# Attention probabilities times values: eight fp32r matmuls a head, or four plain float32 ones over four column quadrants

## The reference

```python
q, k, v = x @ Wq.T, x @ Wk.T, x @ Wv.T          # x is normalised; 16 heads of 32
scores = jnp.where(causal, q k^T / sqrt(32), min)
probs  = softmax(scores)                         # 512 x 512 for each head
attn   = (probs v) @ Wo.T
mod    = 0.1 * tanh(attn @ A)                    # A: 512 x 16
gate   = silu(h @ W_in.T + mod * (h @ A) @ B)
out    = residual + tanh(g) * ((gate * (h @ W_up.T)) @ W_down.T)
```

## Time and profile before

| | before |
|---|---|
| median of 3 runs | 1038.49 us (1037.32 to 1039.15) |
| the profiled execution | 1034.66 us, its span 1032.9 us |
| PE busy | 1005.7 us (97%) |
| DVE busy | 702.4 us (68%) |
| ACT busy | 603.7 us (58%) |
| POOL busy | 279.2 us (27%) |
| granted clock of PE | 1.0 of full speed in the profile |

### The profile page before, as it was taken

One profiled execution on the slowest core, in us unless ns is written; L12 is line 12 of the kernel. 1 busy time (PEld: TensorE's weight loads), 2 busy tenths in 40 slices (PEclk: granted clock), 3 DMA queues, 4 the chain that ended last, 5 costly groups with the idle time before them and its releaser, 6 DMA issues.

```text
span 1032.9 us, 16779 instructions
## 1 busy us (share of the span) xinstructions
PE 1005.7 (97%) x5140; PEld 830.0 (80%) x5141; DVE 702.4 (68%) x1841; ACT 603.7 (58%) x1447; POOL 279.2 (27%) x276
## 2 busy tenths in 40 slices
PE   6999999999999999999999999999999999999998
PEld 5787888777888888778888888778888887888886
DVE  7866755996665559985665489966655599754443
ACT  4564456997444448985344379963444499843332
POOL 4536124861000117640000148600001187300000
PEclk9999999999999999999999999999999999999999
DMA  6635133344222416434332354343234254222221
GB/s 231 216 141 173 41 122 93 83 93 163 93 91 91 132 54 184 95 104 153 96 92 91 112 158 94 77 165 96 94 98 148 57 159 100 85 82 91 91 91 52
DMA packets 47073, 115.78 MB, mean 112 GB/s; under 512 B 6800, under 2 KB 6800, under 8 KB 46096
## 3 DMA queue, kind: packets, MB, share of 16 engines
q1 hardware_dynamic: 43968, 105.06, 34.1%
q0 software_dynamic: 3040, 9.96, 2.8%
HBM read 76.46 MB, written 13.37 MB: 87 GB/s over the span
## 4 chain that ended last, share of the span: by engine, by line
PE 87%; DVE 4%; POOL 3%; DMA 3%; issue 2%; ACT 1%; SPq 1%; DVEq 0%
PE bank L537 67%; PE bank L734 6%; PE bank L797 6%; PE bank L700 3%; DMA stack<-wr 2%; POOL big L493 2%; PE bank L839 1%; PE bank L851 1%; DVE big L1405 1%; PE bank L593 1%; PE bank L768 1%; PE bank L608 1%; PE bank L651 1%; SPq L321 1%; DVE wr L1391 0%
## 5 line engine op out<-in xcount | busy, mean ns | idle before, releaser
L537 PE MATMUL bank<-hT,wr 128*128 128x512 f32 x1488 | 358.0, 390 | 0.0
L537 PEld LDWEIGHTS bank<-hT,wr 128*128 128x128 f32 x1488 | 279.2, 188 | 60.7 <-issue 1.6
L537 PE MATMUL bank<-wr,actr 128*128 128x512 f32 (+1 forms) x1224 | 301.6, 396 | 2.3 <-DVE actr L1373 1.5
L537 PEld LDWEIGHTS bank<-wr,actr 128*128 128x128 f32 x1224 | 227.8, 189 | 50.4 <-issue 3.0
L493 POOL TENSOR_SCALAR big<-big,rr 128x256 f32<-128x256 f32 (+1 forms) x124 | 149.2, 1212 | 76.1 <-DVE rr L1411 75.7
L432 POOL TENSOR_TENSOR wqs<-wstage,wqs 128x512 fp32r<-128x512 f32 x32 | 43.3, 1362 | 436.3 <-ACT wqs L953 435.0
L1436 DVE SCALAR_TENSOR_TENSOR wr<-stream,lns,wr 128x256 fp32r<-128x256 f32 x256 | 121.7, 536 | 52.2 <-ACT wr L1065 52.2
L1038 ACT ACTIVATE big<-big,nb 128x512 f32<-128x512 f32 (+3 forms) x256 | 140.6, 560 | 9.3 <-DVE nb L1405 9.3
L1391 DVE TENSOR_TENSOR wr<-bank,wr 128x512 fp32r<-128x512 f32 (+1 forms) x224 | 125.7, 607 | 19.3 <-ACT wr L953 18.6
L953 ACT ACTIVATE wr<-bank 128x512 fp32r<-128x512 f32 (+1 forms) x224 | 110.3, 529 | 33.5 <-PE bank L537 20.8
L953 ACT ACTIVATE actr<-act_sb 128x512 fp32r<-128x512 f32 x64 | 40.4, 632 | 146.0 <-DVE act_sb L1450 146.0
(11 more groups left out here) (174 smaller groups left out, 990.3 us busy)
## 6 DMA issues: line engine op xcount, KB each, us to landing
stream<-in_wmlp SPq DMA_DIRECT2D x64, 512.0 KB, 4.0
stack<-wr SPq DMA_DIRECT2D x192, 128.0 KB, 2.3
stream<-in_wmlp SPq DMA_DIRECT2D x64, 256.0 KB, 2.7
big<-in_x SPq DMA_DIRECT2D x4, 1024.0 KB
big<-y_rows SPq DMA_DIRECT2D x4, 1024.0 KB, 5.6
residual<-big SPq DMA_DIRECT2D x4, 1024.0 KB
big<-residual SPq DMA_DIRECT2D x4, 1024.0 KB, 6.5
out<-big SPq DMA_DIRECT2D x3, 1024.0 KB, 4.8
```

Of the source, the lines that this page charges most:

```text
L537: mm = pe.matmul(dst, lhs(pl, k), rhs(pr, k), start=start and i == 0, stop=stop and i == n - 1, skip_group_check=skip)
```

## The change

The attends become plain float32 matmuls. For head n and block `kt` of keys the weights are 32 columns of the plain values (16 of this head, and 16 of the next, whose products are not used), and the result goes to partitions 32q to 32q+31 of bank 7 with q = (kt + head) mod 4, that is, to one of four column quadrants of the array: 4 matmuls a head instead of 8. The turned probabilities are copied once and not split, banks 6 and 4 by ACT and bank 5 by DVE, into two sets of buffers. Row block 0 is scaled by DVE instead of ACT, and Pool no longer splits values.

The step on PE becomes: scores of head n+3, all four; filling, if the head is 7 or later; attend head n; turn head n+1; filling, if the head is under 7. DVE's step becomes: scale head n+1, copy bank 5 of head n, maxima of head n+3 (before: n+2, ahead of the low parts). At the end ACT copies all of bank 7 to `ysb`, and one more plain float32 matmul with a 128x16 matrix of ones and zeros (`gather_rows`, made once in the expert stage) adds the quadrants into bank 1; it stands between two halves of chunk 0's gate product. The load of the next batch's y rows waits for the last attend, because a set of turned buffers lies in the same memory.

```diff
-NORM_DVE, NORM_ACT, NORM_POOL = (3,), 0, (1, 2)
-LAST_DVE, LAST_POOL = (3, 2), (1,)
+NORM_DVE, NORM_POOL = (3, 0), (1, 2)
+LAST_DVE, LAST_POOL = (3, 0, 2), (1,)
 POOL_ROWS = len(NORM_POOL) * (H - 1) + len(LAST_POOL)
 TURN_ORDER = (2, 1, 3, 0)
-TURNED_BANKS = ((6, 256, 1024), (5, 512, 512), (4, 512, 0))
+QUADRANTS = 4
...
+        vp_rows = flat[:, 6656:6656 + TT * H * R].rearrange("p (t c) -> p t c", t=TT)
...
+        turned = [{4: act_sb[:, :], 5: sil[:, :], 6: xi[:, 0:256]},
+                  {4: flat[:, 3328:3840], 5: flat[:, 7680:8192], 6: flat[:, 3840:4096]}]
...
-                sp.wait_ge(p_turned, b * (H * 3))
+                sp.wait_ge(pv_done, b * H)
...
-                if not first and kt != 3:
-
-                    pe.wait_ge(pt_lo, (n - 1) * 3 + PART_OF[kt])
+                if not first and kt == 1:
+                    pe.wait_ge(pt_dve, n)
+                elif not first and kt != 3:
+
+                    pe.wait_ge(pt_act, n * 2 - (kt == 2))
                 for qt in range(kt, TT):
...
             def filling(b, head):
 
-                project_part(b, head + 1)
+                if head < H - 1:
+                    project_part(b, head + 1)
...
-                elif head >= LOW_RANK_FROM:
+                elif LOW_RANK_FROM <= head < H - 1:
...
-                def attend(kt, part):
-                    _, _, at = TURNED[kt]
-                    at_row = 64 * (j // 2) + R * (j % 2)
-                    return pe.matmul(bank[ATT][0:3 * R, kt * P:S], vst[:, q % 2, kt, at_row:at_row + 3 * R],
-                                     pts[:, j % 2, part, at:at + S - kt * P], start=head == 0 and kt == 0 and part == HI, stop=False,
-                                     skip_group_check=True)
-
+                def attend(kt, begin, end, quadrant):
+                    bk, col, _ = TURNED[kt]
+                    wide = R * min(2, H - head)
+                    return pe.matmul(bank[ATT][32 * quadrant:32 * quadrant + wide, begin:end],
+                                     vp_rows[:, kt, R * head:R * head + wide],
+                                     turned[j % 2][bk][:, col + begin - kt * P:col + end - kt * P],
+                                     start=head == 0, stop=False, skip_group_check=True)
+
+                def attend_all():
+                    if head == 0:
+                        pe.wait_ge(vpa_ok, b + 1)
+                        pe.wait_ge(vpb_ok, b + 1)
+                    pe.wait_ge(pt_act, n * 2 + 2)
+                    pe.wait_ge(pt_dve, n + 1)
+                    for kt in range(TT):
+                        mm = attend(kt, kt * P, S, (kt + head) % QUADRANTS)
+                    mm.then_inc(pv_done, 1)
+
+                if head < H - 3:
+                    scores(n + 3, other, stack_loads(b, head + 3))
+                if head >= QH * 2 - 1:
+                    filling(b, head)
+                attend_all()
                 if head < H - 1:
                     wait_probs(n + 1)
                     for kt in TURN_ORDER:
                         turn_tiles(n + 1, other, kt)
-                if head < H - 3:
-                    pe.wait_ge(nb_ok, (n + 3) * 4 - 1)
-                    score_rows(other, 2, True)
-                    score_rows(other, 0, False)
-                if head < H - 1:
-                    first, second, third, last = (0, 1, 3, 2) if head == 0 else TURN_ORDER
-                    if j == 0:
-                        pe.wait_ge(vst_lo, b * NQ + q + 1)
-                    attend(first, HI)
-                    if head < H - 3:
-                        pe.wait_ge(nb_ok, (n + 3) * 4)
-                        score_rows(other, 1, True)
-                    attend(first, LO)
-                    for kt in (second, third, last):
-                        attend(kt, HI)
-                        mm = attend(kt, LO)
-                    mm.then_inc(pv_done, 1)
...
+            def gate_part(par, part):
+
+                n = DT * len(PARTS) // 2
+                for i in range(part * n, part * n + n):
+                    k, (pl, pr) = i // len(PARTS), PARTS[i % len(PARTS)]
+                    pe.matmul(bank[GATE[par]][:, :], wch[:, par, pl, k * P:k * P + P], hT[:, pr, k, :],
+                              start=i == 0, stop=False)
...
-                scores_last(b * H + 3, 1, stack_loads(b, 3))
                 for q in range(NQ):
                     for j in range(QH):
                         head_step(b, q, j)
 
                 pe.wait_ge(nb_ok, (b + 1) * H * 4)
-                gate_product(0)
+                gate_part(0, 0)
+                pe.wait_ge(at_low, b + 1)
+                pe.wait_ge(rows_made, 1)
+                pe.matmul(bank[SUM][0:R, :], gather_rows[:, :], ysb[:, :], start=True, stop=True).then_inc(at_sum, 1)
+                gate_part(0, 1)
                 pe.wait_ge(cg_hi, b * NCH + 2)
                 pe.wait_ge(cg_lo, b * NCH + 2)
-
-                pe.wait_ge(at_sum, b + 1)
...
-                for i, (bk, w, at) in enumerate(TURNED_BANKS):
-                    act.wait_ge(p_turned, n * 3 + i + 1)
-                    copy(pts[:, j % 2, HI, at:at + w], bank[bk][:, 0:w]).then_inc(pt_hi, 1)
-                    if i == 0 and (q < NQ - 1 or j < QH - 1):
-                        normalise(n + 1, q * QH + j + 1)
+                act.wait_ge(p_turned, n * 3 + 1)
+                copy(turned[j % 2][6], bank[6][:, 0:256]).then_inc(pt_act, 1)
+                act.wait_ge(p_turned, n * 3 + 3)
+                copy(turned[j % 2][4], bank[4][:, :]).then_inc(pt_act, 1)
...
-                copy(att_low, bank[ATT][32:32 + R, :]).then_inc(at_low, 1)
+                copy(ysb[:, :], bank[ATT][:, :]).then_inc(at_low, 1)
                 act.wait_ge(at_sum, b + 1)
-                a.activation(att_low, att_sum, ACT.Tanh).then_inc(mod_ok, 1)
+                a.activation(att_low, bank[SUM][0:R, :], ACT.Tanh).then_inc(mod_ok, 1)
...
-                one_more, two_more = q < NQ - 1 or j < QH - 1, q < NQ - 1 or j < QH - 2
-                n = (b * NQ + q) * QH + j
-                if one_more:
+                head = q * QH + j
+                n = b * H + head
+                if head < H - 1:
                     normalise(n + 1, (j + 1) % 2)
+                if head == 0:
+                    maxima(n + 2, 0)
                 if (q, j) in COPY_AT:
                     qk_low(b, *COPY_AT[q, j])
-                if two_more:
-                    maxima(n + 2, j % 2)
-                for i, (bk, w, at) in enumerate(TURNED_BANKS):
-                    dve.wait_ge(pt_hi, n * 3 + i + 1)
-                    low(pts[:, j % 2, LO, at:at + w], bank[bk][:, 0:w], pts[:, j % 2, HI, at:at + w], pt_lo)
+                dve.wait_ge(p_turned, n * 3 + 2)
+                v.tensor_copy(turned[j % 2][5], bank[5][:, :]).then_inc(pt_dve, 1)
+                if head < H - 3:
+                    maxima(n + 3, (j + 1) % 2)
...
-                dve.wait_ge(at_low, b + 1)
-                v.tensor_tensor(att_sum, bank[ATT][0:R, :], att_low, ALU.add).then_inc(at_sum, 1)
...
+                elif i == 5:
+                    v.tensor_reduce(gather_rows[:, :],
+                                    ident[:, :].rearrange("p (k r) -> p r k", k=QUADRANTS)[:, 0:R, :], AXX,
+                                    ALU.add).then_inc(rows_made, 1)
```

More of the change, by code:

```diff
@@ L1039, in exponentials @@
                                  accum_out=rs[:, par, qt:qt + 1]).then_inc(exp_ok, 1)
-            def normalise(n, head):
-                par = head % 2
-                act.wait_ge(rr_ok, n + 1)
-                rows = prob_rows(head, NORM_ACT)
-                a.activation(rows, rows, ACT.Copy, scale=rr[:, par, NORM_ACT:NORM_ACT + 1]).then_inc(pn_act, 1)
             def head_step(b, q, j):
```

43 lines of the change are left out of this document (7 added, 36 removed).

## The result

The changed kernel takes 1057.97 us in the median (1056.72 to 1059.56), the kernel before 1038.1 beside it (four runs of each): ratio 1.0198, 95% interval 1.0181 to 1.0216. It is 2% slower. The profiled execution has a span of 1057.0 us against 1032.9; PE is busy 1007.4 us, DVE 666.3 (36 less), ACT 558.6 (45 less), Pool 264.0.

A forecast was written before the change was run, and what follows sets the result against it. No engine was far from the edge: PE bound heads with a projection half, DVE the later ones. Per batch 43.3 + 16A = 62.5 against 65.1 us, four times, +4 for loads: -6.4, so 1032 us, range 1010 to 1060.

The forecast's parts named there:

- rival 2: Switching between whole array and quadrants stalls PE, up to 0.24 us a change: 1053 us (1047 to 1061), chance 0.20.
- New waits: Waits the change adds in the attention: 0.85 us at head 15 and 0.8 a batch (0 to 2) elsewhere.
- (b): Heads 7 and 8: PE, without filling, asks for 2.9 us against ACT and DVE at 3.1; allowed 0.8 a batch.
- (c): Scores at the step's head, maxima at its end: scores of n+3 need maxima of n+2; hidden unless DVE is late.
- A = 1.20: PE time per head of the four plain fp32 attends, records overlapping in program order: 1.20 us, range 1.17 to 1.29.
- Rival 1: Attend quadrants run freely, not in program order: A = 0.90 us a head, 1014 us in all, chance 0.18.
- Late heads at PE's own pace: With DVE at 3.1 us a head instead of 3.80, PE sets the late heads' pace: 3.6 us.
- the 5.6 us of waits: PE's waits in a batch's 65.1 us attention, mostly DVE-bound late heads; expected mostly to go, the change's true gain.
- (a): PE attends head 15 right after turning it, with no filling between: 0.85 us of idle PE.
- The sum: Matmul adding the quadrants within the gate product: 0.9 us on PE a batch, the chain to the modulation staying hidden.
- Loads 1.3 us late, +4 us: y rows wait for the last attend, so chunk 2 weights come 1.3 us late in three batches: +4 us, or 0.
- DVE and ACT: Busy time over the whole kernel should fall by some 50 us on DVE and some 60 on ACT.

The follow-up runs named there:

- run 5: Changed kernel with the projected halves copied a head earlier and DVE's low part between its bank 5 copy and the maxima: 1039.11 us, ratio 1.0019.
- run 6: Changed kernel with plain fp32 attends on 128 value columns, whole array, one after the other (attention result wrong): 1103.04 us, ratio 1.0635.
- run 2: Changed kernel with all four attend blocks of a head in one quadrant, same result: 1113.23 us, ratio 1.0735.
- run 7: run 3 with gate and up weights of chunks 2 and 3 loaded ahead of the next batch's y and x rows: 1052.43 us, ratio 1.0143.
- run 3: Changed kernel without the sum matmul; ACT and DVE add two quadrants, the other two are left out: 1057.34 us, ratio 1.0215.
- run 8: run 5 with gate and up weights of chunks 2 and 3 loaded ahead of the next batch's rows, sum kept: 1037.39 us, ratio 1.0002.

## Why the prediction was wrong

It gave 1032 us and faster; it is 1058 and slower. The time lies in the range of 1010 to 1060, near its end, but by luck: that end stood for rival 2 in full, and the cause was another.

- **The step that failed: "New waits", (b) and (c).** It had the scores at the head of the step and the maxima at its end, and asked only whether PE's scores wait for DVE's maxima: "hidden, unless DVE is late". The tie that binds is the other one. DVE waits for PE's scores of the same step (39.8 us in 36 waits), and what is queued behind those maxima on DVE, the low part, makes PE wait 1.03 three times a batch. The prediction named the moved step and not what stands behind the waiting instruction, and it counted DVE's 3.1 us of work as if they could lie anywhere in the period. It allowed 0.8 us a batch for such waits. The steps show, with 4.25 and 3.53 as the free ones and 2.77 (turns, scores, attends) for step 8: 1.25 in step 0, 3.8 in steps 2, 4 and 6, 1.1 in step 8, 0.9 to 1.8 in step 9 (there also for stack loads), 1.3 in steps 13 and 14: over 8 us. Run 5 takes 4.3 to 5.4 us a batch of them out, 19.3 in all, and with them nearly all of the loss, by the place of one low part in DVE's step and its copy a head earlier. The last sign of failure that the prediction named, DVE's order making PE wait for maxima, came close: PE waited for what stood behind them.
- **The attend, A = 1.20, was mis-sized: it is 0.95 to 0.98.** Rival 1's mechanism is the true one: a record waits for its own quadrant and not for the record ahead of it. About 0.86 of the 0.98 is the longest block's two records, and 0.11 is what run 6 does not have behind the attends. The argument "every PE row I read starts in program order" was true of the rows and said nothing on matmuls in different columns. By the sum, A = 0.98 would have given 3.5 us a batch more gain, 1018, so the waits that were missed are larger than the error in the total shows. The two records of one quadrant do not hold up the others. Alone in one quadrant they take 2.27 (run 2), near the 2.15 of the bound.
  The Trainium skill (TensorE: Matmul & The Clock Gate, Part 3, Packing small matmuls) says column tiles start some 4 ns apart and run together: the trace agrees, with four starts within 0.02 us. It also says that matmuls start and end in program order, by which the sum was made. Of the starts that does not hold here: the second record of the 256-column block starts at 194.77, ahead of those of the 384- and 512-column blocks (194.87, 194.97), which come earlier in the program. Of the ends the trace can't say it, because the ends of PE's records are modelled; the semaphore speaks for order. It stands on the 128-column attend, whose two records take 0.41 us together, yet SP, which waits for it, issues the y rows at 248.65 in the first batch, 1.16 after the attends of head 15 began (247.49) and 0.13 after the modelled end of the longest. In run 2, where that attend is the last to run, this distance is 0.08 (262.22, 262.30).
- **Rival 2, the price of the form, is real and small.** It was priced at 0.24 a change, 0.48 a head, with a middle of 0.36. Runs 2 and 6 show 0.25 a head where PE binds: 0.10 before the first attend, 0.11 after the last, 0.05 in the turns. The 0.11 is already inside the 0.98 of the attend; the rest, with 0.07 of the projection, eats the 0.19 by which the attends became cheaper: a free head is 4.25 us after and 4.26 before. So the change as mended in run 5 ends at 1.0019, not ahead. The 0.07 by which the projection became longer (1.41 to 1.48) is also in run 6, 1.47, and so not due to the quadrants; what causes it is open.
  The Trainium skill (TensorEngine Tiling (Array Packing), Key Properties) states that changing the tiling mode drains the engine. The trace shows a cost of this kind, half of the 0.24 that a full record end would have cost, each way.
- **Late heads at PE's own pace:** right. From step 10 they are 3.53 without a wait for a low part, 3.6 expected. But "the 5.6 us of waits mostly go" was wrong: they came back in the early steps.
- **(a) Head 15:** right, 0.69 by the bracket, and 0.94 from where the turns are through (245.49 + 1.06) to the attend at 247.49, for 0.85.
- **The sum:** 0.96 for 0.9. Its cover was not what was reckoned: the chain is entered 0.50 late because the full copy, into `ysb`, waits for the low rank add that reads `ysb`, and PE stands before the sum, not behind the whole chain. The stretch grew by 1.93 from the gate product's start, of which 0.96 is the matmul.
- **Loads 1.3 us late, +4 us:** the lateness was right in kind, but the sum and its wait moved the need by 2.0 instead of 0.9 (from 7.8 us behind the gate product's start, 251.41 - 243.63, to 9.8): 0.15 was left. It is +4.9 without the sum (run 7 against 3), +1.7 with it (run 8 against 5).
- **DVE and ACT:** 36 and 45 us less busy, for 50 and 60. Row block 0's scaling costs DVE 0.42 a head and not 0.2 (reciprocal and two blocks take 1.03, 190.46 to 191.49, against 0.61 with one block in the earlier trace rows). ACT's shortfall was not traced.

## What to carry to other kernels

When a change reorders two engines' steps, write for each instruction of the slower-looking engine what it waits for and what is queued behind it: an engine at 63% busy made PE wait, because an instruction that nobody was waiting for stood in front of one that PE needed. Put work that another engine wants ahead of an operation that waits for that engine. And judge a cheaper instruction by the free step around it: here 0.19 us gained in the attends was lost as 0.18 in their neighbours, which no idle bracket of PE shows.

## What the runs showed of the hardware

- Plain float32 matmuls of four column quadrants run side by side although each is two records: 8 records of a head in 0.98 us against 2.27 in one quadrant. The second records start out of program order (194.77 before 194.87 and 194.97); the semaphore of the last and shortest matmul comes only when the longest is over (248.65 against 248.52).
- Going between whole-array matmuls and matmuls of 32 columns costs about 0.1 us each way on PE: 0.25 us a head, 10.2 us in 64 heads (run 2 against run 6). PE has no bracket for it; the weight load behind the change starts with its matmul (234.44) and not 0.11 ahead of it (232.55 for 232.66).
- A late transfer can lie hidden behind the very cost that one takes away: run 3 removed 1.1 us a batch and gained nothing until the loads were moved.
